# Attention's second matmul in three bf16 products instead of one fp32 product: probabilities and values split into high and low halves

## The reference, cut to what matters

```python
query = qt_c + qt_r                       # 16 heads of 64
key   = kt_c + kt_r
value = heads(ct_kv @ Wu_v_w + Wu_v_b)
attn = jnp.einsum('bhqd,bhkd->bhqk', query, key) / scale
attn = jax.nn.softmax(attn, axis=-1)
out  = jnp.einsum('bhqk,bhkd->bhqd', attn, value)
...
x = x + _layernorm(_L0_attn_ref(_layernorm(x, axis=-1), ...), axis=-1)
x = x + _layernorm(_L0_ffn_ref(_layernorm(x, axis=-1), ...), axis=-1)
```

## Time and profile before

| | us |
|---|---|
| three runs of the kernel | 7718.76, 8081.82, 8483.87 |
| median of the three | 8081.82 |
| the profiled execution | 7727.77 |
| its span, slowest core (core 5) | 7726.2 |
| spans of the eight cores | 7690.5 to 7726.2 |

### The profile page before, as it was taken

The page is one execution under the profiler, slowest core; times in us unless marked ns, Lnnn a source line. Parts: engine busy times, 40 slices in busy tenths (PEclk is TensorE's granted clock), DMA queues, the critical chain, the costliest instruction groups (busy, mean ns, idle before and its releaser), DMA issues.

```text
span 7726.2 us, 74820 instructions; the slowest of 8 cores (7690.5 to 7726.2 us)
## 1 busy us (share of the span) xinstructions
PE 6110.8 (79%) x24080; PEld 2305.3 (30%) x24080; DVE 1861.7 (24%) x3412; ACT 2146.8 (28%) x3157; POOL 187.1 (2%) x445
## 2 busy tenths in 40 slices
PE   3888788688899989998999899993546788777882
PEld 1333333233222222222222222221223333333331
DVE  3433334344011111111111110002223333333323
ACT  1121222021444434443444344441221001000003
POOL 0000000000000000000000000000000000000000
PEclk9999889899999989998999899996768999999986
DMA  4111111310111111111111111112001101111012
GB/s 104 44 55 53 58 55 44 82 42 28 56 46 45 45 52 44 46 46 51 46 45 46 53 46 47 47 44 60 33 31 35 33 20 30 33 33 33 21 30 85
DMA packets 409835, 356.54 MB, mean 46 GB/s; under 512 B 106351, under 2 KB 370543, under 8 KB 409468
## 3 DMA queue, kind: packets, MB, share of 16 engines
q1 hardware_dynamic: 375388, 316.05, 13.5%
q0 software_dynamic: 34080, 35.71, 2.8%
HBM read 294.73 MB, written 75.76 MB: 48 GB/s over the span
## 4 chain that ended last, share of the span: by engine, by line
PE 75%; DVE 10%; DMA 5%; ACT 5%; issue 4%; DVEq 0%; SPq 0%; ACTq 0%; POOL 0%; POOLq 0%
PE pall L288 39%; PE pall L837 23%; PE pall L875 9%; PE pall L880 3%; DVE sq_scr L906 3%; DMA w1h_sb<-w 2%; ACT sq_scr L303 1%; ACT sq_scr L300 1%; DVE hl_sb L1165 1%; DVE xnTh_t L444 1%; ACT ao_t L1157 1%; ACT hh_sb L1162 1%; ACT xn L430 1%; DVE sq_scr L917 0%; DVE ol_t L925 0%
## 5 line engine op out<-in xcount | busy, mean ns | idle before, releaser
L894 ACT ACTIVATE pt<-pall,negM 128x512 f32<-128x512 f32 x2048 | 1402.6, 687 | 1827.0 <-PE pall L837 1335.3
L837 PE MATMUL pall<-pt,vt_sb 128*65 128x512 f32 x4096 | 1866.4, 599 | 0.0
L906 DVE RECIPROCAL sq_scr<-pall 1x512 f32<-1x512 f32 x64 | 214.5, 3351 | 2805.4 <-PE pall L837 2803.8
L837 PEld LDWEIGHTS pall<-pt,vt_sb 128*65 128x65 f32 x4096 | 524.1, 137 | 1117.9 <-issue 1117.9
L880 PE MATMUL pall<-qt_sb,kt_sb 64*128 64x512 bf16 x3072 | 857.0, 388 | 0.0
L875 PE MATMUL pall<-qt_sb,kt_sb 64*128 64x512 bf16 x3072 | 782.1, 390 | 71.0 <-DMA kt_sb<-kT_hbm 54.1
L288 PE MATMUL pall<-xn2Th_sb,w1h_sb 128*128 128x512 bf16 x1024 | 402.0, 393 | 247.5 <-DVE w1l_sb L1114 247.5
L1157 ACT ACTIVATE ao_t<-pall,b_col 128x512 f32<-128x512 f32 x128 | 88.0, 687 | 1540.0 <-PE pall L288 1476.1
L288 PE MATMUL pall<-ident,xn 128*128 128x128 f32 x384 | 93.2, 424 | 496.1 <-ACT xn L430 271.5
L288 PE MATMUL pall<-w2h_sb,hh_sb 128*128 128x512 bf16 x1024 | 391.0, 382 | 117.9 <-DVE hl_sb L1165 117.9
L875 PEld LDWEIGHTS pall<-qt_sb,kt_sb 64*128 64x128 bf16 x3072 | 255.2, 96 | 743.4 <-issue 516.8
(11 more groups left out here) (223 smaller groups left out, 5894.5 us busy)
## 6 DMA issues: line engine op xcount, KB each, us to landing
vt_sb<-v_hbm SPq DMA_DIRECT2D x512, 130.0 KB, 2.1
kt_sb<-kT_hbm SPq DMA_DIRECT2D x512, 128.0 KB, 2.2
xt<-xv SPq DMA_DIRECT2D x48, 512.0 KB, 3.9
v_hbm<-v_t SPq DMA_DIRECT2D x32, 520.0 KB, 2.7
wscr<-w SPq DMA_DIRECT2D x128, 128.0 KB, 2.1
wscr<-w SPq DMA_DIRECT2D x32, 512.0 KB, 3.9
xnT_hbm<-xnTh_t SPq DMA_DIRECT2D x64, 128.0 KB, 2.0
xnT_hbm<-xnTl_t SPq DMA_DIRECT2D x64, 128.0 KB, 1.9
```

The costliest lines, as they stand in the source:

```text
L837: tav = p.do("tensor", lambda e, bufip=bufip, hh=hh, kcp=kcp: e.matmul(PB(hh)[0:65, 0:512], vt_sb[bufip][:, 65 * hh:65 * hh + 65], pt32[:, ...
L894: tex = p.do("scalar", lambda e, sbb=sbb, hh=hh: e.activation(pt32[:, 512 * hh:512 * hh + 512], PB(sbb)[:, 0:512], AF.Exp, bias=negM[:], s ...
L906: trc = p.do("vector", lambda e, hh=hh: e.reciprocal(lrec_row, PB(hh)[64:65, 0:512]), deps=[av_tok[hh], LU.get("lrec_row")])
```

## The change

Values are stored as two bf16 halves, and so are the probabilities. `v_hbm` becomes `[S, 2, 1040]` bf16, with the same bytes in all. In stage A1 each value group gets a second VectorE operation that makes the low half, and each 128 rows go out in two DMAs, the second of which waits for the first. In stage B the exponential still writes float32 `pt32`. For heads 0 and 1 of the four a GpSimd DMA casts `pt32` to `pth`; for heads 2 and 3 VectorE copies it. For each head VectorE then makes `ptl = pt32 - pth`. `pth` and `ptl` have one buffer per head, as `pt32` has. Each head's float32 matmul becomes three bf16 matmuls. All else is unchanged.

```diff
-    v_hbm = nc.dram_tensor("v_hbm", [S, H * 65], F32, kind="Internal").ap()
+    v_hbm = nc.dram_tensor("v_hbm", [S, 2, H * 65], BF16, kind="Internal").ap()
...
-    v_t = asb("v_t", [128, 2 * 1040])
+    vh_t = asb("vh_t", [128, 2 * 1040], BF16)
+    vl_t = asb("vl_t", [128, 2 * 1040], BF16)
...
+    t_vl0 = p.do("gpsimd", lambda e: e.memset(vl_t[:], 0.0))
...
+                tl_ = p.do("vector", lambda e, vh_dst=vh_dst, vl_dst=vl_dst, bkid=bkid:
+                           e.scalar_tensor_tensor(
+                    vl_dst, PB(bkid)[:, 0:512].rearrange("p (h j) -> p h j", j=64), 1.0,
+                    vh_dst, Op.mult, Op.subtract),
+                    deps=[g, th_, t_vl0, LU.get(("vsp", cs))])
...
             tsp = p.do("sync", lambda e, cs=cs, c=c, r0_tile=r0_tile: e.dma_start(
-                out=v_hbm[r0_tile + 128 * c: r0_tile + 128 * c + 128, :],
-                in_=v_t[:, 1040 * cs:1040 * cs + 1040]), deps=ev_t, dma=f"vsp{cs}")
+                out=v_hbm[r0_tile + 128 * c: r0_tile + 128 * c + 128, 0, :],
+                in_=vh_t[:, 1040 * cs:1040 * cs + 1040]), deps=ev_t, dma=f"vsp{cs}")
+            tsp = p.do("sync", lambda e, cs=cs, c=c, r0_tile=r0_tile: e.dma_start(
+                out=v_hbm[r0_tile + 128 * c: r0_tile + 128 * c + 128, 1, :],
+                in_=vl_t[:, 1040 * cs:1040 * cs + 1040]), deps=ev_t + [tsp], dma=f"vsp{cs}")
...
-                    tav = p.do("tensor", lambda e, bufip=bufip, hh=hh, kcp=kcp: e.matmul(
-                        PB(hh)[0:65, 0:512],
-                        vt_sb[bufip][:, 65 * hh:65 * hh + 65],
-                        pt32[:, 512 * hh:512 * hh + 512],
-                        start=(kcp == 0), stop=(kcp == 31)), deps=dd)
+                    for pi, (vf, pf, dtok) in enumerate(
+                            [(vh, ph, thv), (vh, pl_, tlv), (vl, ph, thv)]):
+                        dd = [dtok, tvlp]
...
+                        tav = p.do("tensor", lambda e, vf=vf, pf=pf, hh=hh, kcp=kcp, pi=pi:
+                                   e.matmul(
+                            PB(hh)[0:65, 0:512], vf(), pf(),
+                            start=(kcp == 0 and pi == 0),
+                            stop=(kcp == 31 and pi == 2)), deps=dd)
...
                 tvl = p.do("sync", lambda e, Q=Q, kc=kc, bufi=bufi: e.dma_start(
-                    out=vt_sb[bufi][:],
-                    in_=v_hbm[128 * kc:128 * kc + 128, 260 * Q:260 * Q + 260]),
+                    out=vt_sb[bufi][:].rearrange("p (hl c) -> p hl c", hl=2),
+                    in_=v_hbm[128 * kc:128 * kc + 128, :, 260 * Q:260 * Q + 260]),
...
+                    if hh < 2:
+                        thv = p.do("gpsimd", lambda e, hh=hh: e.dma_start(
+                            out=pth[:, 512 * hh:512 * hh + 512],
+                            in_=pt32[:, 512 * hh:512 * hh + 512]),
+                            deps=[tex], dma=f"pc{hh}")
+                    else:
+                        thv = p.do("vector", lambda e, hh=hh: e.tensor_copy(
+                            pth[:, 512 * hh:512 * hh + 512],
+                            pt32[:, 512 * hh:512 * hh + 512]), deps=[tex])
+                    tlv = p.do("vector", lambda e, hh=hh: e.tensor_tensor(
+                        ptl[:, 512 * hh:512 * hh + 512],
+                        pt32[:, 512 * hh:512 * hh + 512],
+                        pth[:, 512 * hh:512 * hh + 512], Op.subtract),
+                        deps=[thv, tex])
+                    infos.append((hh, thv, tlv))
```

More of the change, by code:

```diff
@@ L484, in build_program @@
             vones.append(p.do("gpsimd", lambda e, c=c, hg=hg: e.memset(
-                v_t[:, 1040 * c + 65 * hg + 64: 1040 * c + 65 * hg + 65], 1.0)))
+                vh_t[:, 1040 * c + 65 * hg + 64: 1040 * c + 65 * hg + 65], 1.0)))
     t_vones = vones[-1]
@@ L600, in build_program @@
                 g = mm_group(bkid, mms, extra_deps=[LU.get(("vev", cs, oh))])
-                vh_dst = v_t[:, 1040 * cs + 520 * oh: 1040 * cs + 520 * oh + 520] \
+                vh_dst = vh_t[:, 1040 * cs + 520 * oh: 1040 * cs + 520 * oh + 520] \
+                    .rearrange("p (h j) -> p h j", j=65)[:, :, 0:64]
+                vl_dst = vl_t[:, 1040 * cs + 520 * oh: 1040 * cs + 520 * oh + 520] \
                     .rearrange("p (h j) -> p h j", j=65)[:, :, 0:64]
@@ L606, in build_program @@
                 bk.read(bkid, th_)
-                ev_t += [th_]
-                LU[("vev", cs, oh)] = th_
-            tsp = p.do("sync", lambda e, cs=cs, c=c, r0_tile=r0_tile: e.dma_start(
-                out=v_hbm[r0_tile + 128 * c: r0_tile + 128 * c + 128, :],
-                in_=v_t[:, 1040 * cs:1040 * cs + 1040]), deps=ev_t, dma=f"vsp{cs}")
+                tl_ = p.do("vector", lambda e, vh_dst=vh_dst, vl_dst=vl_dst, bkid=bkid:
[3 more added lines that the diff above has]
+                    deps=[g, th_, t_vl0, LU.get(("vsp", cs))])
+                bk.read(bkid, tl_)
+                ev_t += [th_, tl_]
+                LU[("vev", cs, oh)] = tl_
+            tsp = p.do("sync", lambda e, cs=cs, c=c, r0_tile=r0_tile: e.dma_start(
+                out=v_hbm[r0_tile + 128 * c: r0_tile + 128 * c + 128, 0, :],
[3 more added lines that the diff above has]
+                in_=vl_t[:, 1040 * cs:1040 * cs + 1040]), deps=ev_t + [tsp], dma=f"vsp{cs}")
             LU[("vsp", cs)] = tsp
@@ L810, in build_program @@
     kt_sb = [bsb(f"kt_sb{i}", [128, 512], BF16) for i in range(2)]
-    vt_sb = [bsb(f"vt_sb{i}", [128, 260]) for i in range(2)]
+    vt_sb = [bsb(f"vt_sb{i}", [128, 2 * 260], BF16) for i in range(2)]
     pt32 = bsb("pt32", [128, 4 * 512])
+    pth = bsb("pth", [128, 4 * 512], BF16)
+    ptl = bsb("ptl", [128, 4 * 512], BF16)
     o32 = [sq_scr[0:64, 512:1024]]
@@ L832, in emit_av @@
                 last = None
[L833 to L836, removed]
-                    tav = p.do("tensor", lambda e, bufip=bufip, hh=hh, kcp=kcp: e.matmul(
-                        PB(hh)[0:65, 0:512],
-                        vt_sb[bufip][:, 65 * hh:65 * hh + 65],
-                        pt32[:, 512 * hh:512 * hh + 512],
-                        start=(kcp == 0), stop=(kcp == 31)), deps=dd)
+                for hh, thv, tlv in infos:
+                    vh = lambda bufip=bufip, hh=hh: vt_sb[bufip][:, 65 * hh:65 * hh + 65]
+                    vl = lambda bufip=bufip, hh=hh: vt_sb[bufip][:, 260 + 65 * hh:
+                                                                  260 + 65 * hh + 65]
+                    ph = lambda hh=hh: pth[:, 512 * hh:512 * hh + 512]
+                    pl_ = lambda hh=hh: ptl[:, 512 * hh:512 * hh + 512]
+                    tav = None
+                    for pi, (vf, pf, dtok) in enumerate(
+                            [(vh, ph, thv), (vh, pl_, tlv), (vl, ph, thv)]):
+                        dd = [dtok, tvlp]
+                        if kcp == 0 and pi == 0:
+                            dd = dd + bk.pre_write(hh)
+                        tav = p.do("tensor", lambda e, vf=vf, pf=pf, hh=hh, kcp=kcp, pi=pi:
[3 more added lines that the diff above has]
+                            stop=(kcp == 31 and pi == 2)), deps=dd)
                     if kcp == 0:
@@ L898, in build_program @@
                     bk.read(sbb, tex)
-                    infos.append((hh, tex))
+                    if hh < 2:
[13 more added lines that the diff above has]
+                    infos.append((hh, thv, tlv))
                 pend = (kc, bufi, tvl, infos)
```

## The result

The changed kernel is slower: the ratio of its time to that of the kernel before is 1.043, 95% interval 1.040 to 1.046. Its profiled execution took 8054.67 us (span 8053.1) where the one before took 7727.77 (7726.2): +327 us.

A forecast was written before the change was run, and what follows sets the result against it. The prediction took TensorE's matmul time to bound the kernel. Its terms, 16 x (32 x (6.1 - 5.42) + 6.6) = 454 plus 25 for stage A1, made 479 us on 7726.2: 8205 us, range 7890 to 8800.

The forecast's parts named there:

- Rival 2: Whole kernel faster: TensorE goes on setting stage B's period, 4.4 us a pass, 7337 us; chance 0.04.
- the loop over two passes: Stage B: VectorE's queue, AV 3, scores, AV 0, exponentials, issue: 8.8 us plus landing over two passes, 5.5 to 5.7 each.
- steady pass, less 5.42: Stage B key loop: period rises from 5.42 to 6.1 us in each of 16 x 32 passes.
- start and end of a block: Each of 16 `qt` blocks in stage B: first AV +4.8 us, block end +1.8, together 6.6, nothing hidden.
- stage A1, a tile (x8): End of each A1 tile: last subtraction 0.69 us and second store's wait some 2.4; 3.1 x 8 = 25 us.
- I charge half of that, 0.4: Stage B, each pass: 0.4 us for loads meeting casts, half of 0.8 for a full meeting.
- the loop of head 0: Stage B: exponential, GpSimd issue, landing, subtraction, three products, next exponential: 5.70 us, before the charge for meetings.
- The last term: Head 0's loop in stage B: AV to next exponential, 3 x 0.215 on the array plus 0.3 behind it, 0.96 us.
- Rival 1: No change within 2%: landing near its floor, nothing meets it, stage B period 5.46, 7880 us; chance 0.10.
- Rival 3: Stage B cast costs what the weights' casts cost: landing 4.1, period 7.15, 8745 us; chance 0.12.
- Rival 5: Clock falls: matmuls at 1.2 GHz make stage B's pass TensorE's own 7.7 us, 9025 us; chance 0.07.
- Rival 4: Stage B: GpSimd's issue waits for one VectorE cast a pass, +0.42, period 6.5, 8420 us; chance 0.07.

The follow-up runs named there:

- e1: Changed kernel with two buffers for the float32 probabilities and both bf16 halves, used by even and odd passes: 7548.05 us, 0.976 of the kernel before.
- e2: Changed kernel with all four heads cast by VectorE, none by GpSimd DMA, single buffers: 7386.28 us, 0.955 of the kernel before.
- e4: Changed kernel loading keys and values only in the first two passes of each block (wrong keys): 8018.06 us, median period 5.57.
- e3: Changed kernel with heads 2 and 3 treated before heads 0 and 1, loads kept: median period 6.0 to 6.1 us; no whole time compared.
- e5: e3 with keys and values loaded only in passes 0 and 1 of each block: median period 5.20 to 5.26 us; no whole time compared.
- e9: Changed kernel with one GpSimd DMA cast (head 0) and three casts on VectorE, single buffers: 8015.12 us, median period 5.65.

## Why the prediction was right or wrong

**Direction and kind of mechanism: right.** The AV of a head now ends a loop with a landing in it, and that outlasts the matmul time saved. e1 and e2 show it from both sides: loosen the loop with a second buffer (4.60), or take the landing out of it (4.55). Which of the two loops sets the period, and one charge on it, were wrong; see below. Rival 2 (TensorE goes on setting the period, 4.4) is wrong for this kernel, and for e1 too: its 4.60 lies near 4.4, but its timeline shows the loop over two passes, and TensorE can do a pass in 4.12.

**The size: too large on the execution that it was made against.** 479 us were forecast there (+6.2%) and 327 measured; 8054.67 us lies inside the range of 7890 to 8800. The measured ratio is +4.3%. Told against the median of 8081.82 the same forecast of 8205 us reads +1.5%, too small by far: the prediction gave both percentages, but that median and the profiled execution are not of one clock, and only the 6% can be set against the ratio. By terms, in us:

| term | forecast | measured | in all: forecast, measured |
|---|---|---|---|
| steady pass, less 5.42 | 0.68 | 0.25 | 348, 128 |
| start and end of a block | 6.6 | 8.5 | 106, 136 |
| stall of GpSimd | none | 2.4 | 0, 38 |
| stage A1, a tile (x8) | 3.1 | 3.6, half of it hidden | 25, 15.5 |

**The step that failed: "I charge half of that, 0.4"** for loads that meet the casts. It is 16 x 32 x 0.4 = 205 us of the 479, more than the whole error. e4 puts it at 0.05 us in this order of heads, 26 us in all. The premise, that both share every pass, says nothing of when in the pass: the loads wait for the tile that the last AV and scores free, the casts are issued 1.6 us earlier and land in 2.3. e3 and e5 show that a meeting does cost, twice what was charged, when it takes place. Without the charge the period would have read 5.7 and the sum 274 us. That 5.7 is close to the 5.68 measured, but for the loop of head 0, from which it was summed, this is luck: that loop was 0.4 too long, as follows.

**The loop's own terms.** Exponential 0.69, result to issue 0.56 and subtraction 0.69 were right: head 0's exponential, 0.69 from 3207.73, ends at 3208.42, and the issue is at 3208.95. The landing is 2.3 (2.48 to the subtraction), not 2.43 (2.65). The Trainium skill, "DMA: Bandwidth & Descriptors", "Anatomy of one DMA", has a fixed 2.0 us and bytes over 436e3; as an estimate that gives 2.3 with the 131,072 bytes written and 2.6 with the 262,144 read. The measured 2.3 agrees with the former, loosely: for the 65,536 bytes of the earlier trace rows the same formula gives 2.15, and 1.9 was measured. The last term was counted wrong: of AV's 0.96, the first of three products needs only `pth` and can run beside the subtraction. Counted so, the loop is 0.69 + 0.56 + 2.48 + 0.69 + 0.15 + 2 x 0.215 + 0.3 = 5.30, under 5.42. By itself it would not have made the kernel slower.

What holds the period above it is the loop over two passes, forecast at 5.5 to 5.7: 5.49 with the median landing, 5.70 as the trace has it. The two take turns. Over all eight cores, the next exponential of head 0 follows the end of head 0's subtraction by 0.84 us, its least, in 37% of the passes: there the short loop ended last. In the pass that holds 3217.30, whose landing was late, it did. In the other 63% TensorE was still held by the scores, that is, by the long loop. The median of all is 5.62. The long loop explains e9 as well: from head 0's subtraction to the end of head 3's, VectorE's queue takes 4.1 us with one DMA head and 3.9 with two, and behind it stands a landing in either.

**Block ends.** The start was forecast fairly well. The casts do stand behind the output moves:

```profile
3110.65 2.55 ACT L917 ACTIVATE pt<-pall,negM 128x512 f32<-128x512 f32 x4 [34.49 <-PE pall L903]
...
3115.02 0.52 POOL L969 DMA_DIRECT2D OTl_sb<-ol_t  x1 [2.62 <-DMA OTh_sb<-oh_t]
3115.53 1.11 POOL L923 DMA_DIRECT2D pth<-pt  x2
3118.08 1.49 DVE L931 TENSOR_TENSOR ptl<-pt,pth 128x512 bf16<-128x512 f32 x2 [6.75 <-DMA pth<-pt]
3120.05 0.69 ACT L917 ACTIVATE pt<-pall,negM 128x512 f32<-128x512 f32 x1 [6.85 <-PE pall L861]
```

The first exponential ends at 3110.65 + 0.69 = 3111.34 and its cast is issued 4.2 us later; the first period grows by 3.9 us (4.8 forecast). The other end is the one that was short: +5.0 for the last pass and what follows it, where 0.68 + 1.8 were forecast. In the last pass nothing overlaps the issue, the landing and VectorE's queue; e2, the same kernel without the DMA casts, has 38.7 there, so some 2.2 of the 5.0 are the DMA; the rest I put down to VectorE's queue, which no run shows apart.

**Stage A1.** The load is issued 3.3 us after the last VectorE operation, not 0.45; with the subtraction it is 3.6 a tile (3.1 forecast). Of 8 x 3.6 = 29, 15.5 reached the end of the stage: about half must be hidden behind other work, where the prediction took none. What hides it was not looked for.

**The other rivals.** Rival 1 had the landing near its floor of 2.1 and a period of 5.46: the landing is 2.48 by that count, and the whole is 4.3% over, not within 2%. Rival 3 is wrong by the rows: the landing is 2.3 and not 4.1, although shape and operation are those of the weights' casts. Those come from HBM and share their moment with loads; which of the two makes them slow no run tells. Rival 5 is wrong as well: the clock stayed at 0.91.

Rival 4 asked whether GpSimd's issue has to wait for a cast of VectorE. Issues and casts do overlap, as here, where the cast ends at 3214.46 and the issue above starts at 3214.41:

```profile
3214.04 0.42 DVE L928 CAST pth<-pt 128x512 bf16<-128x512 f32 x1
```

Counted over core 7 of the changed kernel: in 153 passes a cast of VectorE was running when the issue for head 0 started, and the issue came 0.54 us after the exponential's end, as in the other 343. The 179 issues that overlap a cast by more than 0.1 us (0.34 in the middle) last 0.548 us in the mean against 0.529 for the rest, and their casts land no later (2.29 against 2.33). The price is 0.02 us, not 0.42. The stall that the Trainium skill, "SBUF — State Buffer", "Who interferes with whom", describes does not show in this trace.

## What to carry to other kernels

Before a step is moved to an engine or queue that looks idle, ask which buffer's loop it enters: with one buffer the whole latency counts (here 3 us for a cast that takes 0.42 us on VectorE), and whether one or two such transfers stand in a pass hardly does. Follow the loop over two passes too, through the order in which an engine takes its work: a second buffer does not cut that one. Follow each product to the operand that it really needs, and each transfer to its moment in the pass; a shared queue is no meeting. Where the loop can't be shortened, double the buffer first, and see which engine's sum then sets the period.

## What the runs showed of the hardware beyond that

- A 128 x 512 float32 to bf16 DMA from SBUF to SBUF lands in 2.3 us when the loads of a pass come 1.6 us after it or not at all, and in 3.1 in the median when two loads of about 128 KB are issued within 0.5 us of it; the key load then takes 3.2 instead of 2.4 (e3 against the changed kernel).
- GpSimd, with steady DMA issues, is late by some 1.8 us once in 72 issues (changed kernel), or by 2.9 us once in 120 (e9); the cause is open.
- A second Exp from the same bank, written as bf16 (0.687 us), was the cheapest way to a high half here, as ScalarE had room.
